# Summing the states of a state-space layer by accumulating transposes

## The chip, the cores and the metric

The kernel runs on one core of a Trainium2 chip. The metric is device time in microseconds. PE is the matrix engine (PEld its weight loads), DVE the vector engine, ACT the scalar engine, POOL is GpSimd and SP issues DMAs. An engine works through its own queue in order; semaphores tie the queues together.

## The reference

A small language model on 64 sequences of 128 tokens, 192 channels, all float32: embedding and layer norm, attention, a mixture of experts, a bidirectional state-space layer, a second mixture of experts, each added to the residual. The change is in the state-space layer:

```
xp, z = split(x @ W_in.T)                  # 384 channels each
xc = silu(causal_conv(xp, 4 taps) + conv_b)
dt, B, C = split(xc @ W_xproj.T)           # 12, 16, 16
dt = softplus(dt @ W_dt.T + b_dt);  A = -exp(A_log)
h[t] = exp(dt[t] * A) * h[t-1] + (dt[t] * xc[t]) * B[t]     # 384 x 16 states
y[t] = sum over the 16 states of h[t] * C[t]
y = (y + xc * D) * silu(z)
out = y @ W_out.T
layer = 0.5 * (forward over x + the same over x reversed)
```

## The kernel before

The phases follow one another; the state-space layer is `mamba_phase`. It works in 16 groups of 4 sequences (512 tokens). A group has a forward half (d = 0) and a backward half (d = 1), a half has 16 states n, and a state has three chunks c of 128 channels. The 48 pairs (n, c) of a half are its units, counted by p. Channels lie on the partitions, the 512 tokens along the free axis.

In each unit ACT writes the decays exp(dt A) into one of four PSUM banks (`act_decay`, L1760; `RING` says which), POOL has written u times B for the whole state into one of eight buffers xh (`pool_dBx`, L1804, two states ahead), and the DVE runs the recurrence as a scan (L1773). Then h is multiplied by C: for the states listed in `BY_POOL` (8 in the forward half, 6 in the backward half) POOL does it for the whole state in one call (`pool_read`, L1793), for the others the DVE does it chunk by chunk (`dve_read`, L1784). PE adds the product into the bank that holds y for the chunk, through a product with the identity (`pe_sum`, L1731), three states behind. D times xc goes into the same bank as a product with a diagonal matrix (`pe_D`, L1724). Both halves of a group add into these banks. When a group is complete, the DVE multiplies each chunk by silu(z) into ys (`dve_y`, L1811), PE multiplies ys by W_out (`pe_out`, L1743), and the DVE adds that to the residual H (`dve_out`, L1816).

While a half runs, the next half is prepared in between: `chain` puts the layer norm, the input product, the gate (L1561, L1562, copied by ACT at L1568), the convolution (L1579), the projection (L1599) and the softplus onto the engines at the units named in `POS`. The softplus ends in a loop over four engines. ACT makes e = exp(-|x|) (L1632) and two more tensors; POOL issues a DMA that adds e to r (`pool_add`, L1651); for each chunk PE sums three tensors through the identity (`pe_sp`, L1666), ACT copies the sum to dt (L1671), the DVE makes u = dt xc (L1675), and PE takes the next chunk only after u of the one before. One PSUM bank (`NB`) serves all these products. POOL needs u of all three chunks for the first product of the next half.

The order of each engine's queue is written out by hand: in each unit p first the main work, then what `POS` puts there (on PE what `POS` puts there first). POOL's main work in a state n is the product of state n+2, and then the read of state n-1 if it is POOL's.

Of the kernel before, what the change touches and what calls it, by code (L numbers as in the profile page):

```python
# [15 lines left out]
P = 128  # L16
# [3 lines left out]
G = 4  # L20
# [1334 lines left out]
def mamba_phase(nc, A, H, bank, K, Y, BCd, W):  # L1355
# [5 lines left out]
    with Phase(nc) as ctx:  # L1361
# [5 lines left out]
        POS = {  # L1367
            "y": (6, 7, 9), "pe_D0": (14, 15, 17), "pe_D1": (6, 16, 25), "pe_out": (17, 18), "out": (14, 15),
            "act_rows": (11, 13), "rows": (12, 14), "stats": 14, "rstd": 18, "norm": 40,
# [7 lines left out]
        NB = 7  # L1377
        BY_POOL = (0, 3, 4, 5, 10, 12, 13, 14), (0, 6, 9, 10, 11, 14)
        RING = ((3, 4, 5, 6) * 2 + (3, 4, 5, 3, 4, 5, 3) + (6, 4, 5, 3) * 8 + (6,),
# [54 lines left out]
        s_er, = ctx.software(K, 1)  # L1434
        s_gy, s_ops, s_out = sem("gated_ready"), sem("outps_ready"), sem("res_ready")

        def seqs(t):
# [24 lines left out]
        def act_gz(act, g):  # L1462
            act.wait_ge(s_zc, g * DC + DC)
            act.activation(gz[:, :, :], gz[:, :, :], ACT.Silu).then_inc(s_gz, 1)
# [8 lines left out]
        def chain(g, d, norm=True, first=False):  # L1473
# [57 lines left out]
            def act_zT(act, i):  # L1531
                if i == 0 and not first:
                    act.wait_ge(s_zps, gl * DC)
                act.wait_ge(s_zTps, gl * 2 + 1 + i)
                if i == 0:
                    act.copy(zTa[:, :], bank[:, front(i), :]).then_inc(s_zT, 1)
                else:
                    act.copy(zTb, bank[0:CR, front(i), :]).then_inc(s_zT, 1)
# [15 lines left out]

            def pe_gate(pe, c):
                if c == 0:
                    pe.wait_ge(s_abs, (s + 1) * 2 * DC)
                else:
                    pe.wait_ge(s_zc, g * DC + c)
                m = slice((DC + c) * P, (DC + c + 1) * P)  # L1560
                pe.matmul(bank[:, front(c), :], win_a[:, m], zTa[:, :], start=True, stop=False)  # L1561
                pe.matmul(bank[:, front(c), :], win_b[:, m], zTb, start=False, stop=True).then_inc(s_zps, 1)  # L1562

            def act_gate(act, c):
                act.wait_ge(s_zps, g * DC + c + 1)
                if c == 0 and deep:
                    act.wait_ge(s_gy, g * DC)
                act.copy(gz[:, c, :], bank[:, front(c), :]).then_inc(s_zc, 1)  # L1568

# [84 lines left out]
            def pe_sp(pe, c):  # L1654
                if c == 0:
                    if d == 1:
                        pe.wait_ge(s_zc, g * DC + DC)
                        stand_alone(pe, K.go)
                    pe.wait_ge(s_nc, s + 1)
                elif not first:  # L1660
                    pe.wait_ge(s_u, s * DC + c)
# [31 lines left out]
            for name, on_pe, on_act in stages:  # L1693
                if name == "x" and d == 1 or name == "gate" and d == 0:
                    continue
                for c in range(DC):
                    put("pe", POS[f"pe_{name}{d}"][c], on_pe, c)
                    put("act", POS[f"act_{name}{d}"][c], on_act, c)
# [19 lines left out]
        def pe_D(pe, g, d, c):  # L1718
            pe.wait_ge(s_xc, g * 2 + d + 1)
            if d == 0 and later(g):  # L1720
                pe.wait_ge(s_gy, (g - 1) * DC + c + 1)
            elif d == 0:
                pe.wait_ge(s_u, DC)
            pe.matmul(bank[:, c, :], dgD[:, c, :], xc[d][:, c, :], start=(d == 0), stop=False).then_inc(s_D, 1)  # L1724

        def pe_sum(pe, g, d, n, c):
            if n not in BY_POOL[d]:
                pe.wait_ge(s_prv, dve_reads(g, d, n) + c + 1)
            elif c == 0:
                pe.wait_ge(s_prp, pool_reads(g, d, n + 1))  # L1730
            mm = pe.matmul(bank[:, c, :], K.ident[:, :], xh[n % NX][:, c, :], start=False, stop=(d == 1 and n == NS - 1))  # L1731
            mm.then_inc(s_red, 1)

        def pe_out(pe, g, i):
            if i == 0:
                pe.wait_ge(s_gy, g * DC + DC)
                if not (isinstance(g, int) and g == NG - 1):
# [69 lines left out]
        def dve_y(dve, g, c):  # L1807
            dve.wait_ge(s_red, (g * 2 * NS + 2 * NS - 1) * DC + c + 1)
            if c == 0:
                dve.wait_ge(s_gz, g + 1)  # L1810
            dve.tensor_tensor(ys[:, c, :], bank[:, c, :], gz[:, c, :], ALU.mult).then_inc(s_gy, 1)  # L1811

# [84 lines left out]
        with nc.Block() as block:  # L1897
            @block.tensor
            def _(pe):
                def main(pe, g, d, p, end):  # L1900
                    carry = d == 0 and later(g)
                    if carry and p in POS["pe_D0"]:
                        pe_D(pe, g, d, POS["pe_D0"].index(p))
# [9 lines left out]
                def after(pe):  # L1913
                    for n in range(NS - LAG, NS):
                        for c in range(DC):
                            pe_sum(pe, NG - 1, 1, n, c)
                    for i in two:
                        pe_out(pe, NG - 1, i)
# [3 lines left out]
            def _(act):  # L1922
                def main(act, g, d, p, end):
                    act_decay(act, g, d, p)
                program(act, "act", main, lambda act: None, lambda act: None)

# [135 lines left out]
```

## Time and profile before

| | us |
|---|---|
| runs: median (lowest to highest of 3) | 4718.52 (4717.42 to 4736.08) |
| profiled execution, its span from first to last instruction | 4718.1 |
| PE busy | 4271.6 (91%) |
| DVE busy | 3251.1 (69%) |
| POOL busy | 3212.3 (68%) |
| ACT busy | 2430.7 (52%) |

The profile shows one execution. Busy time says how long an engine worked, not that it was needed: an engine that waits in order for another may be the last link of a loop although it has gaps. The state-space layer runs from about 1210 to 3818 us.

### The profile page before, as it was taken

The page shows a single profiled execution, that of the slowest core. Times are in us where ns is not written, and L with a number is a line of the kernel's source. Part 1 is how long each engine was busy: PE and PEld are TensorE (multiplying, and loading weights), DVE is VectorE, ACT ScalarE, POOL GpSimd, SP SyncE. Part 2 cuts the span into 40 slices and gives each one's busy share as a digit, 9 for nine tenths or more (in the row PEclk, how much of TensorE's full clock was granted, in tenths as well). Part 3 has the DMA queues.
Part 4 walks back from the last instruction along what each step waited for, and adds up shares of the span by engine and source line. Part 5 has one row for each costly group of instructions (what it writes and reads, how often), then busy time and mean ns, then how long its engine had stood idle before and what let it go on. Part 6 is the DMA issues. An engine that isn't in the chain of part 4 may idle for free. (4 is left out here: it accounts for less than half of the span.)

```text
span 4718.1 us, 62490 instructions
## 1 busy us (share of the span) xinstructions
PE 4271.6 (91%) x16896; PEld 2235.4 (47%) x16896; DVE 3251.1 (69%) x5016; ACT 2430.7 (52%) x4880; POOL 3212.3 (68%) x1669
## 2 busy tenths in 40 slices
PE   7999986997899999999999999999999876999994
PEld 4666644664343443344334434433443334666673
DVE  5667773111699999999999999989999975111114
ACT  3555542122566666767676666667666633222221
POOL 3222222442799999999999999999999941444441
PEclk9999996998899999999999999999999987999997
DMA  1000011342334333334333333333333321333456
GB/s 35 21 20 20 20 53 59 108 127 76 107 114 125 115 118 116 121 109 121 122 112 115 112 121 118 116 118 113 117 107 123 114 67 45 110 116 112 127 169 219
DMA packets 267113, 478.79 MB, mean 101 GB/s; under 512 B 39404, under 2 KB 176444, under 8 KB 266908
## 3 DMA queue, kind: packets, MB, share of 16 engines
q1 hardware_dynamic: 235776, 403.02, 26.9%
q0 software_dynamic: 28032, 73.17, 6.1%
q14 instruction: 171, 1.40, 0.1%
q10 hardware_dynamic: 3100, 0.64, 0.1%
q8 instruction: 34, 0.56, 0.1%
HBM read 409.75 MB, written 41.81 MB: 96 GB/s over the span
## 5 line engine op out<-in xcount | busy, mean ns | idle before, releaser
L1804 POOL TENSOR_TENSOR m_xh<-m_u,m_Bb 128x1536 f32<-128x1536 f32 x512 | 1780.1, 3550 | 51.6 <-DVE m_u L1675 39.0
L1731 PE MATMUL bank<-m_xh,ident 128*128 128x512 f32 x3072 | 1455.1, 609 | 34.3 <-POOL m_xh L1793 34.3
L1773 DVE TENSOR_TENSOR_SCAN bank<-bank,m_xh 128x512 f32<-128x512 f32 x864 | 1038.9, 1216 | 44.5 <-ACT bank L1760 42.2
L1760 ACT ACTIVATE bank<-m_dt,m_Ac 128x508 f32<-128x508 f32 x1536 | 1024.9, 683 | 38.4 <-DVE m_xh L1773 38.4
L1731 PEld LDWEIGHTS bank<-m_xh,ident 128*128 128x128 f32 x3072 | 576.2, 194 | 820.0 <-issue 730.7
L1773 DVE TENSOR_TENSOR_SCAN m_xh<-bank,m_xh 128x512 f32<-128x512 f32 x672 | 787.8, 1207 | 64.8 <-ACT bank L1760 59.3
L1793 POOL TENSOR_TENSOR m_xh<-m_xh,m_Cb 128x1536 f32<-128x1536 f32 x224 | 794.0, 3544 | 4.3 <-DVE m_xh L1773 4.0
L1784 DVE TENSOR_TENSOR m_xh<-bank,m_Cb 128x512 f32<-128x512 f32 x864 | 581.3, 673 | 10.9 <-DMA m_Cb<-BC_rows 10.8
L1204 ACT ACTIVATE f1t_h<-bank,f1t_b 128x512 f32<-128x512 f32 (+1 forms) x276 | 147.6, 586 | 509.9 <-PE bank L1234 509.9
L1134 POOL DMA_INDIRECT rows_y<-f1t_y,f1t_home x142 | 139.9, 985 | 316.4 <-DVE f1t_y L1175 287.1
L1579 PE MATMUL bank<-m_xp,m_dg 128*128 128x512 f32 x768 | 351.9, 601 | 3.7 <-DVE m_u L1675 1.4
L1243 PE MATMUL bank<-f1t_w,f1t_h 128*128 128x192 f32 x1704 | 289.0, 329 | 19.4 <-ACT f1t_h L1204 19.4
L1243 PEld LDWEIGHTS bank<-f1t_w,f1t_h 128*128 128x128 f32 x1704 | 275.7, 190 | 31.6 <-issue 28.1
L1759 ACT COPY bank<-m_none 128x4 f32<-128x4 f32 x896 | 144.2, 161 | 260.5 <-DVE m_xh L1784 171.3
L1164 DVE COPY f1t_xTa<-bank 128x512 f32<-128x512 f32 (+1 forms) x46 | 26.2, 570 | 342.2 <-PE bank L1215 342.2
L97 POOL TENSOR_SCALAR ln_e_ve<-ln_e_mv 128x4 f32<-128x4 f32 x16 | 3.7, 229 | 348.2 <-DVE ln_e_mv L91 348.2
L1579 PEld LDWEIGHTS bank<-m_xp,m_dg 128*128 128x128 f32 x768 | 142.9, 190 | 201.6 <-issue 157.0
L373 DVE TENSOR_REDUCE mx<-bank 128x3 f32<-128x384 f32 x256 | 141.0, 551 | 113.4 <-PE bank L552 112.1
L1231 PE MATMUL bank<-f1t_xTa,f1t_w1a 128*128 128x512 f32 (+1 forms) x552 | 217.1, 516 | 1.6 <-DVE f1t_xTb L1167 1.6
L1175 DVE TENSOR_TENSOR f1t_y<-bank,f1t_b 128x192 f32<-128x192 f32 x142 | 50.8, 358 | 216.7 <-PE bank L1243 216.7
L1204 ACT ACTIVATE f0t_h<-bank,f0t_b 128x512 f32<-128x512 f32 (+1 forms) x132 | 71.9, 596 | 246.5 <-PE bank L1234 246.5
L454 ACT COPY ST<-bank 128x384 f32<-128x384 f32 x256 | 120.8, 472 | 143.0 <-PE bank L562 143.0
(367 smaller groups left out, 6148.3 us busy)
## 6 DMA issues: line engine op xcount, KB each, us to landing
m_Bb<-BC_rows SPq DMA_DIRECT2D x256, 512.0 KB, 4.8
m_Cb<-BC_rows SPq DMA_DIRECT2D x256, 512.0 KB, 4.0
f1t_w<-f_w SPq DMA_DIRECT2D x46, 576.0 KB
m_r<-m_dt POOLq DMA_DIRECT2D x32, 768.0 KB, 7.4
f1t_w1a<-f_w SPq DMA_DIRECT2D x46, 384.0 KB
f0t_w<-f_w SPq DMA_DIRECT2D x22, 576.0 KB
f1c_yg<-rows_y SPq DMA_DIRECT2D x16, 768.0 KB, 8.3
f1t_w1b<-f_w SPq DMA_DIRECT2D x92, 96.0 KB
```

The lines of the kernel that those rows point to most:

```text
L373: dve.reduce_max(mx[:, u % NE, :], s_ps, AX).then_inc(s_mx, 1)
L1204: act.activation(h[b][:, m, 0:w * P], bank[:, HB[(s2 + m) % 4], 0:w * P], ACT.Gelu, bias=b1[b][:, m:m + 1]).then_inc(s_gelu, 1)
L1231: pe.matmul(o[f], w1a[b][:, (m + f) * P:(m + f + 1) * P], xTa[b][:, 0:w * P], start=True, stop=False)
L1243: mm = pe.matmul(bank[:, YB[j % 2], 0:C], h[b][:, m, j * P:(j + 1) * P], w2[b][:, m, :], start=(m == 0), stop=(m == HK - 1))
L1579: mm = pe.matmul(bank[:, front(c), :], dg[:, c, k, :], xp[:, c, :, o:o + P], start=(k == 0), stop=(k == TAPS - 1))
L1731: mm = pe.matmul(bank[:, c, :], K.ident[:, :], xh[n % NX][:, c, :], start=False, stop=(d == 1 and n == NS - 1))
L1759: act.copy(o[:, :, edge:edge + 1], none[:, :].unsqueeze(2))
L1760: act.activation(o[:, :, lo:hi], seqs(dt[d][:, c, :])[:, :, lo:hi], ACT.Exp, scale=Ac[:, c, n:n + 1]).then_inc(s_dA, 1)
L1773: dve.tensor_tensor_scan(o, bank[:, RING[d][p], way], xh[n % NX][:, c, way], 0.0, ALU.mult, ALU.add).then_inc(s_h, 1)
L1784: dve.tensor_tensor(xh[n % NX][:, c, :], bank[:, RING[d][p], :], Cb[q % RC][:, n % QN, :], ALU.mult).then_inc(s_prv, 1)
L1793: pool.tensor_tensor(v, v, Cb[q % RC][:, n % QN, :].unsqueeze(1).to_broadcast([P, DC, TOK]), ALU.mult).then_inc(s_prp, 1)
L1804: pool.tensor_tensor(xh[n % NX][:, :, :], u[d][:, :, :], Bb[q % RB][:, n % QN, :].unsqueeze(1).to_broadcast([P, DC, TOK]), ALU.mult).then_ ...
```

## The change

The sum over the states is turned. PE now takes each 128 x 128 block of the product as the stationary operand and adds its transpose into the bank, so that y lies with tokens on the partitions and channels along the free axis. D is added in that layout (xc stationary, the diagonal matrix moving), and the gate is computed in it (z's tokens stationary, W_in moving, one step for each of the four sequences). The DVE multiplies y by the gate in place in gz. Since the output product needs channels on the partitions, PE then turns the gated product back (`pe_yT`) and ACT copies it to ys (`act_yT`). The waits on ys move from `s_gy` to the new semaphore `s_ys`. GpSimd reads out 7 and 5 states instead of 8 and 6: state 13 of the forward half and state 10 of the backward half go to the DVE.

```diff
@@ -1365,17 +1365,17 @@
         POS = {
-            "y": (6, 7, 9), "pe_D0": (14, 15, 17), "pe_D1": (6, 16, 25), "pe_out": (17, 18), "out": (14, 15),
+            "y": (6, 7, 9), "pe_yT": (8, 9, 11), "act_yT": (10, 11, 13), "pe_D0": (14, 15, 17), "pe_D1": (6, 16, 25), "pe_out": (17, 18), "out": (14, 15),
             "act_rows": (11, 13), "rows": (12, 14), "stats": 14, "rstd": 18, "norm": 40,
             "pe_zT": (43, 46), "act_zT": (44, 45), "pe_x0": (0, 1, 2), "act_x0": (0, 1, 4), "pe_conv0": (3, 4, 5),
-            "act_conv0": (6, 10, 12), "pe_conv1": (0, 2, 4), "act_conv1": (1, 4, 7), "pe_gate1": (23, 26, 31), "act_gate1": (25, 27, 30),
+            "act_conv0": (6, 10, 12), "pe_conv1": (0, 2, 4), "act_conv1": (1, 4, 7), "pe_gate1": (23, 25, 27, 31), "act_gate1": (24, 26, 28, 32),
             "pe_dt0": (12, 14, 16), "act_dt0": (17, 20, 22), "pe_dt1": (20, 21, 22), "act_dt1": (19, 21, 22), "pe_pj": (10, 11),
...
         NB = 7
-        BY_POOL = (0, 3, 4, 5, 10, 12, 13, 14), (0, 6, 9, 10, 11, 14)
+        BY_POOL = (0, 3, 4, 5, 10, 12, 14), (0, 6, 9, 11, 14)
         RING = ((3, 4, 5, 6) * 2 + (3, 4, 5, 3, 4, 5, 3) + (6, 4, 5, 3) * 8 + (6,),
@@ -1433,6 +1433,7 @@
         s_gy, s_ops, s_out = sem("gated_ready"), sem("outps_ready"), sem("res_ready")
+        s_yT, s_ys = sem("gated_turned"), sem("gated_copied")
 
@@ -1460,7 +1461,7 @@
         def act_gz(act, g):
-            act.wait_ge(s_zc, g * DC + DC)
+            act.wait_ge(s_zc, g * G + G)
             act.activation(gz[:, :, :], gz[:, :, :], ACT.Silu).then_inc(s_gz, 1)
@@ -1530,7 +1531,7 @@
                 if i == 0 and not first:
-                    act.wait_ge(s_zps, gl * DC)
+                    act.wait_ge(s_zps, gl * G)
                 act.wait_ge(s_zTps, gl * 2 + 1 + i)
@@ -1552,20 +1553,20 @@
 
-            def pe_gate(pe, c):
-                if c == 0:
+            def pe_gate(pe, j):
+                if j == 0:
                     pe.wait_ge(s_abs, (s + 1) * 2 * DC)
                 else:
-                    pe.wait_ge(s_zc, g * DC + c)
-                m = slice((DC + c) * P, (DC + c + 1) * P)
-                pe.matmul(bank[:, front(c), :], win_a[:, m], zTa[:, :], start=True, stop=False)
-                pe.matmul(bank[:, front(c), :], win_b[:, m], zTb, start=False, stop=True).then_inc(s_zps, 1)
-
-            def act_gate(act, c):
-                act.wait_ge(s_zps, g * DC + c + 1)
-                if c == 0 and deep:
-                    act.wait_ge(s_gy, g * DC)
-                act.copy(gz[:, c, :], bank[:, front(c), :]).then_inc(s_zc, 1)
+                    pe.wait_ge(s_zc, g * G + j)
+                o, sl = bank[:, NB, 0:DC * P], slice(j * P, (j + 1) * P)
+                pe.matmul(o, zTa[:, sl], win_a[:, DC * P:2 * DC * P], start=True, stop=False)
+                pe.matmul(o, zTb[:, sl], win_b[:, DC * P:2 * DC * P], start=False, stop=True).then_inc(s_zps, 1)
+
+            def act_gate(act, j):
+                act.wait_ge(s_zps, g * G + j + 1)
+                if j == 0 and deep:
+                    act.wait_ge(s_yT, g * DC)
+                act.copy(gz[:, :, j * P:(j + 1) * P], bank[:, NB, 0:DC * P].rearrange("p (c x) -> p c x", c=DC)).then_inc(s_zc, 1)
 
@@ -1654,7 +1655,7 @@
                     if d == 1:
-                        pe.wait_ge(s_zc, g * DC + DC)
+                        pe.wait_ge(s_zc, g * G + G)
                         stand_alone(pe, K.go)
@@ -1693,7 +1694,7 @@
                     continue
-                for c in range(DC):
+                for c in range(G if name == "gate" else DC):
                     put("pe", POS[f"pe_{name}{d}"][c], on_pe, c)
@@ -1718,22 +1719,39 @@
             if d == 0 and later(g):
-                pe.wait_ge(s_gy, (g - 1) * DC + c + 1)
+                pe.wait_ge(s_ys, (g - 1) * DC + c + 1)
             elif d == 0:
                 pe.wait_ge(s_u, DC)
-            pe.matmul(bank[:, c, :], dgD[:, c, :], xc[d][:, c, :], start=(d == 0), stop=False).then_inc(s_D, 1)
+            for j in range(G):
+                sl = slice(j * P, (j + 1) * P)
+                mm = pe.matmul(bank[:, c, sl], xc[d][:, c, sl], dgD[:, c, :], start=(d == 0 and j == 0), stop=False, skip_group_check=True)
+            mm.then_inc(s_D, 1)
 
...
                 pe.wait_ge(s_prp, pool_reads(g, d, n + 1))
-            mm = pe.matmul(bank[:, c, :], K.ident[:, :], xh[n % NX][:, c, :], start=False, stop=(d == 1 and n == NS - 1))
+            for j in range(G):
+                sl = slice(j * P, (j + 1) * P)
+                mm = pe.matmul(bank[:, c, sl], xh[n % NX][:, c, sl], K.ident[:, :], is_transpose=True, start=False,
+                               stop=(d == 1 and n == NS - 1), skip_group_check=True)
             mm.then_inc(s_red, 1)
+
+        def pe_yT(pe, g, c):
+            pe.wait_ge(s_gy, g * DC + c + 1)
+            for j in range(G):
+                sl = slice(j * P, (j + 1) * P)
+                mm = pe.transpose(bank[:, c, sl], gz[:, c, sl], K.ident[:, :])
+            mm.then_inc(s_yT, 1)
+
+        def act_yT(act, g, c):
+            act.wait_ge(s_yT, g * DC + c + 1)
+            act.copy(ys[:, c, :], bank[:, c, :]).then_inc(s_ys, 1)
 
...
             if i == 0:
-                pe.wait_ge(s_gy, g * DC + DC)
+                pe.wait_ge(s_ys, g * DC + DC)
                 if not (isinstance(g, int) and g == NG - 1):
@@ -1808,7 +1826,7 @@
                 dve.wait_ge(s_gz, g + 1)
-            dve.tensor_tensor(ys[:, c, :], bank[:, c, :], gz[:, c, :], ALU.mult).then_inc(s_gy, 1)
+            dve.tensor_tensor(gz[:, c, :], bank[:, c, :], gz[:, c, :], ALU.mult).then_inc(s_gy, 1)
 
@@ -1899,6 +1917,8 @@
                     carry = d == 0 and later(g)
+                    if carry and p in POS["pe_yT"]:
+                        pe_yT(pe, g - 1, POS["pe_yT"].index(p))
                     if carry and p in POS["pe_D0"]:
@@ -1914,6 +1934,8 @@
                             pe_sum(pe, NG - 1, 1, n, c)
+                    for c in range(DC):
+                        pe_yT(pe, NG - 1, c)
                     for i in two:
@@ -1922,7 +1944,13 @@
                     act_decay(act, g, d, p)
-                program(act, "act", main, lambda act: None, lambda act: None)
+                    if d == 0 and later(g) and p in POS["act_yT"]:
+                        act_yT(act, g - 1, POS["act_yT"].index(p))
+
+                def after(act):
+                    for c in range(DC):
+                        act_yT(act, NG - 1, c)
+                program(act, "act", main, lambda act: None, after)
 
```

## Rows read from the trace of the kernel before

**Rows 1.** The page's first line.

```profile
span 4718.1 us, 62490 instructions
```

**Rows 2.** Windows over the state-space phase; the sum and mean of 16 stretches.

```profile
core 0: us, PE busy (x) PEld busy (x) DVE busy (x) ACT busy (x) POOL busy (x), PEclk, DMA share, GB/s
...
sum 2608.00, PE 2495.93 PEld 1035.06 DVE 2390.08 ACT 1727.46 POOL 2555.50; mean PE 156.00 PEld 64.69 DVE 149.38 ACT 107.97 POOL 159.72
```

**Rows 3.** Groups by line and shape, 1860 to 3480 us: busy us, mean ns | idle before.

```profile
L1804 POOL TENSOR_TENSOR m_xh<-m_u,m_Bb 128x1536 f32<-128x1536 f32 x319 | 1109.7, 3552 | 20.4 <-DVE m_u L1675 11.6 <-PE bank L1731 8.7
...
L1784 DVE TENSOR_TENSOR m_xh<-bank,m_Cb 128x512 f32<-128x512 f32 x537 | 361.3, 673 | 5.4 <-DMA m_Cb<-BC_rows 5.3
...
L1568 ACT COPY m_gz<-bank 128x512 f32<-128x512 f32 x30 | 17.5, 584 | 6.6 <-PE bank L1562 6.4
```

**Rows 4.** Timeline of the DVE: start us, us, instruction, count [idle before <-releaser].

```profile
1875.74 0.69 DVE L1811 TENSOR_TENSOR m_r<-bank,m_gz 128x512 f32<-128x512 f32 x1 [1.86 <-PE bank L1731]
...
2338.13 0.69 DVE L1675 TENSOR_TENSOR m_u<-bank,m_xc 128x512 f32<-128x512 f32 x1
...
2399.17 0.67 DVE L1784 TENSOR_TENSOR m_xh<-bank,m_Cb 128x512 f32<-128x512 f32 x1
2399.76 1.22 DVE L1773 TENSOR_TENSOR_SCAN bank<-bank,m_xh 128x512 f32<-128x512 f32 x1
...
2420.76 0.69 DVE L1675 TENSOR_TENSOR m_u<-bank,m_xc 128x512 f32<-128x512 f32 x1 [1.71 <-ACT m_dt L1671]
...
2501.70 0.69 DVE L1675 TENSOR_TENSOR m_u<-bank,m_xc 128x512 f32<-128x512 f32 x1 [0.16 <-ACT m_dt L1671]
...
2687.47 0.69 DVE L1811 TENSOR_TENSOR m_r<-bank,m_gz 128x512 f32<-128x512 f32 x1 [1.78 <-PE bank L1731]
```

**Rows 5.** Timeline of POOL, 2336 to 2503 us.

```profile
2336.36 10.41 POOL L1804 TENSOR_TENSOR m_xh<-m_u,m_Bb 128x1536 f32<-128x1536 f32 x3
2346.57 3.61 POOL L1793 TENSOR_TENSOR m_xh<-m_xh,m_Cb 128x1536 f32<-128x1536 f32 x1
...
2396.50 0.90 POOL L1651 DMA_DIRECT2D m_r<-m_dt  x1
...
2421.75 3.44 POOL L1804 TENSOR_TENSOR m_xh<-m_u,m_Bb 128x1536 f32<-128x1536 f32 x1 [0.51 <-DVE m_u L1675]
...
2473.55 0.88 POOL L1651 DMA_DIRECT2D m_r<-m_dt  x1
...
2502.67 3.45 POOL L1804 TENSOR_TENSOR m_xh<-m_u,m_Bb 128x1536 f32<-128x1536 f32 x1 [0.81 <-DVE m_u L1675]
```

**Rows 6.** Timeline of ACT, e of the softplus.

```profile
2467.14 1.48 ACT L1632 ACTIVATE m_dt<-m_dt 128x1536 f32<-128x1536 f32 x1
```

**Rows 7.** Waits, 1860 to 3480 us (ten groups): us in total, times, longest.

```profile
ACT m_dt L1671 <- PE bank L1666: 165.0, 59, 5.0
```

**Rows 8.** Timeline of PE: softplus sums, state sums, transposes, products of 70 columns.

```profile
2411.36 1.02 PE L1666 MATMUL bank<-m_u,ident 128*128 128x512 f32 x2
...
2413.08 1.02 PE L1666 MATMUL bank<-m_r,ident 128*128 128x512 f32 x2
2413.94 3.60 PE L1731 MATMUL bank<-m_xh,ident 128*128 128x512 f32 x8
...
2421.60 0.63 PE L1528 MATMUL bank<-ident,m_z 128*128 128x128 f32 x4 [0.63 <-DVE m_u L1675]
...
2481.09 1.99 PE L1666 MATMUL bank<-m_r,ident 128*128 128x512 f32 x2 [3.53 <-DMA m_r<-m_dt]
...
747.90 27.37 PE L1037 MATMUL bank<-f0v_marked,f0v_at_lo 128*128 128x70 f32 x127 [13.29 <-DVE f0v_at_lo L1000]
```

**Rows 9.** Windows, granted clock third from last: PE alone; all engines; L562's transposes alone.

```profile
2481.00:2483.50 2.50, 2.41 (x3) 0.53 0.27 110
...
750.00:755.00 5.00, 5.00 (x25) 5.00 (x25) 1.88 (x2) 2.82 (x12) 0.00 (x0) 0.50 0.02 3
...
155.00:255.00 100.00, 22.67 (x129) 15.13 (x129) 0.98 0.07 20
```

## The prediction

> **What bounds the kernel now.** I read the page first: the span is 4718.1 us [rows 1]. The windows by stretch come next: the state-space phase fills 2608 us, and cut into 16 stretches of 163 us on the mean, about a group each, it has POOL busy 159.7, PE 156.0 and DVE 149.4 us, ACT only 108 [rows 2]. So three engines are near full, and an average can't say which one paces. The groups by line give the prices [rows 3]: one POOL call on a state (three chunks of 512) takes 3.55 us, one DVE read of a chunk 0.673. The timelines give the order. From the first gated product of one group to that five groups later the DVE takes 811.73 us, 162.35 a group [rows 4], and that is the number to move.
>
> Why 162.35? The softplus hides a loop through all engines. POOL issues the DMA that adds into r; PE needs r for the first softplus sum; ACT copies it and meanwhile issues no decays; the DVE waits for decays and for u; POOL can't begin the next half's products before u's third chunk. In the cycle that I follow, third u chunks begin at 2338.13, 2420.76 and 2501.70: half A (82.6 us) and half B (80.9 us) [rows 4]. On POOL both halves are nearly gapless: calls start every 3.40 us, from (10.21 / 3) [rows 5], and the r DMA is issued at 2396.50 and 2473.55 in the middle of the queue. In half B ACT had e ready at 2467.14 + 1.48 = 2468.6 [rows 6], so the DMA stood 4.9 us behind POOL's earlier calls. POOL waits only 0.5 and 0.8 us for u at the half's end [rows 5]: POOL and the softplus loop finish together.
>
> PE is late too, but through its queue: ACT waits 165 us in ten groups for softplus sums behind other work [rows 7]. The DVE waits 1.71 us for the third u chunk of half A, and 1.86 (first of six groups) to 1.78 us (last) for the first gated product [rows 4].
>
> **Part by part, for one group.**
> (1) GpSimd. Readouts of state 13 forward and state 10 backward leave POOL: 2 x 3.40 = 6.80 us. By the issue order (the product of state n+2, then the read of n-1) both belong to half B: the read of 13 stands behind the first product of the next half, the read of 10 behind the DMA. Half A keeps its 23 calls: 23 x 3.40, the DMA 0.7 and the layer norm's small steps, some 2.3 = 81.2 us. In half B the DMA comes one call, 3.40 us, earlier.
> (2) DVE. Six more reads at the spacing of a read, 2399.76 - 2399.17 = 0.59 us [rows 4]: 3.5 us. Busy becomes 152.9 of 162.35. In half B three reads (state 10) lie between the r DMA and the third u chunk, on the loop: +1.77. One of state 13's lies before half A's last chunk, where POOL is later anyway; two open half B, +1.2, within the 4.9 - 3.40 = 1.5 us that ACT's e still has in hand before the DMA.
> (3) PE sums. Now 2 records per sum, spaced (3.60 - 0.61) / 7 = 0.43 us [rows 8]: 0.855 a sum, 96 sums 82 us. New: four 128-column transposes. The program's own transposes are one record each, four of them 0.63 us; with 0.28 for the last, a spacing of 0.117 [rows 8]. Four make 0.47, 96 sums 45 us, a saving of 37. Bounds: 0.28 x 4 = 1.12 a sum if they don't overlap at all (25 us more than now, which would make PE the bound), and 0.855 if accumulating transposes run as two passes like a plain float product. I take 0.47, the same operation in the same phase.
> (4) D: 4 products of 128 columns, two records each; 8 x 0.117 = 0.94 against 0.855 (no overlap: 8 x 0.28 = 2.24), six a group, +0.5 us of PE (up to +8). The gate: 6 x 2 records of 512 columns become 8 x 2 of 384, the same columns. The turn back of y: 12 transposes, 1.4 us. PE's sum: 156.0 - 37 + 0.5 + 1.4 = 121 us.
> (5) ACT: three new copies of 128x512 at 0.584, as the gate's copies [rows 3], 1.75 us; four gate copies of 384 columns instead of three of 512 (same elements, one more start, below 0.6 us). ACT has 54 us idle.
> (6) Waits. PE now waits for the gated product before each turn, ACT for the turn, PE's D for the copy. Behind PE's wait stand the last sum, the projection and D; behind ACT's copies the decays of units 11 to 13. Through D and the output product the DVE's residual add may come about 1 us later than now. All of it lies in the first part of half A, before the r DMA, where POOL's queue is the later one. It costs nothing as long as that holds, about 1 us a group when it doesn't. DMAs, SP's queue and the waits for B and C rows are unchanged in count; C rows are released by the reader of the state, sooner or later by under a call.
>
> **Sum.** Half A: POOL still has 81.2 us; with 0.3 for the hop from u to POOL 81.6 (now 82.6 here). Softplus in A gains more than this (the 1.71 us wait goes with PE's backlog), but POOL holds it. Half B: 80.94 - 3.40 (call) + 1.77 (reads) - 0.7 (small waits for u behind PE's queue) = 78.6; if PE also starts r's sum at full clock, 0.9 less, 77.7. This sum took 1.99 us in half B at 2481.09 against the usual 1.02 (at 2413.08), after PE had waited 3.53 us for the DMA, with a granted clock of 0.53 in that stretch, the 1.2 GHz level for most of it [rows 8, 9]. So a cycle of 159.3 to 160.2, say 159.85 against the mean 162.35: 2.5 us. Over 15 cycles 38 us. The last half, all POOL's, loses two calls (6.8 us), of which the DVE's reads give back half, and the drain gains a turn and a copy: -3 net, an estimate from the same prices. 4718.1 - 38 - 3 = 4677 us. Span and run agree (4718.1 against the median 4718.52), so the 0.4 us around the span is kept as nothing.
>
> **The clock.** PE will have some 40 us of slack a group in place of 6, in short gaps. In this trace a wait of 3.5 us was followed by 0.53 [rows 9]. A run of products of 70 columns, each with a new 128-column load, stayed at 1.2 GHz (0.50) although PE was never idle in its 27.37 us (127 records, 0.216 apart) [rows 8, 9]. New sums also load 128 columns for each 128 that they move. Against it: the attention stage gives 22.67 of 100 us to transposes and is granted 0.98 [rows 9]. But there they lie among products, so the row decides nothing about long runs. The Trainium skill, page "TensorE: Matmul & The Clock Gate", section "Part 4: PE-mode transpose", says that the full clock does not come on for transposes. By that rule sum runs would go at 1.2 GHz and the fourth rival below would hold; no run here shows it for a transpose yet.
>
> **Rivals.**
> Second: the DVE becomes the bound and gives the gain back. For it: it takes over 3.5 us, and of its 13 us idle only the two waits on PE (1.8 and 1.71) are plainly PE's: 162.35 + 3.5 - 3.5 gives 162.35, with the drain 4717. Against it: its waits in half B follow from the late DMA, which comes earlier.
> Third: POOL was the only bound, and all 6.8 us show: 15 x 6.8 + 4 = 106, 4612. Against it: half A keeps its 23 calls.
> Fourth, slower: PE at 1.2 GHz in the softplus stretches. Its place is the loop: the second and third softplus sums are 2.58 us each at full clock (2411.36 to 2413.94 [rows 8]) and wait for the u before them, so at half rate each adds 2.58 us to the loop. Half A: 5.1 more, less some 2 that its loop has in hand against POOL once the 1.71 us wait is gone, +3; half B: +5. 159.85 + 8 = 168, +5.5 a group against now, 4718 + 83 = 4800. It decides from 2.5 us a group on, that is when nearly half of these sums run slow. If PE ran slow all the time, (156 - 82) x 2 + 96 x 0.94 = 238 us a group, far above; the worst end, which I don't reach, since bursts of plain products follow in each half.
> Fifth: accumulating transposes cost two passes. PE stays at 158; only POOL's call and the DVE's reads count, some 1.6 us a group, 4695.
>
> **How the numbers follow.** Forecast 0.44 (own range 4655 to 4700), second 0.20, third 0.14, fourth 0.16, fifth 0.06. Within 0.5% (4694.5 to 4741.7), about what a measurement can tell from no change: a tenth of the first, most of the second and half of the fifth. Faster: nine tenths of the first, all of the third, rest of the fifth and some of the second, 0.59. Slower: most of the fourth, 0.15. Same: 0.26. The range reaches from between the third and the first to the foot of the fourth: 4625 to 4750.
>
> **What would show it.** Right: 32 + 12 POOL calls a group, half A still about 81 us with gapless POOL, half B below 79; sum records near 0.117 us apart; PE near 121 us busy a group; the wait of the first gated product for PE gone. Wrong: granted clock well below 0.9 in this phase with softplus sums near 5 us; or DVE busy above 155 us a group with POOL waiting for scans; or two records per transpose.

## The result, and the profile after

The changed kernel takes 4796.39 us (median, 4794.92 to 4799.32) against 4723.32 for the kernel before (four runs, the three of the table above and one more): ratio 1.0155, 95% interval 1.0142 to 1.0168. It is slower by 73 us, where 38 + 3 us less were forecast. In the profiled executions the spans are 4793.6 and 4718.1 us [rows 1], 75.5 apart.

The page of the kernel after: the busy line and the clock that TensorE was granted, in 40 slices.

```profile
span 4793.6 us, 70708 instructions
...
PE 3905.7 (81%) x20800; PEld 2516.5 (52%) x20800; DVE 3303.5 (69%) x5112; ACT 2480.3 (52%) x5040; POOL 3113.2 (65%) x1637
...
PEclk9999997997898989998899988989999877999997
```

Windows of the kernel after over the state-space phase, the sum and mean of 16 stretches of a group each, which answers to [rows 2]:

```profile
sum 2685.00, PE 2129.53 PEld 1317.16 DVE 2444.14 ACT 1778.42 POOL 2455.99; mean PE 133.10 PEld 82.32 DVE 152.76 ACT 111.15 POOL 153.50
```

POOL fell by 6.2 us a group and the DVE rose by 3.4, both as forecast (two calls less, six reads more). PE fell by 22.9, not 35. No engine fills its stretch of 167.8 us as POOL did before: POOL is busy for 91% of it, where it was 98%.

Timeline of the DVE after (start, duration, instruction, idle before it): the first gated products four groups apart, and u's chunks in the cycle from 2378 to 2547 us. It answers to [rows 4].

```profile
1899.47 0.69 DVE L1829 TENSOR_TENSOR m_gz<-bank,m_gz 128x512 f32<-128x512 f32 x1 [0.98 <-PE bank L1737]
...
2378.39 0.68 DVE L1676 TENSOR_TENSOR m_u<-bank,m_xc 128x512 f32<-128x512 f32 x1
...
2449.83 0.69 DVE L1676 TENSOR_TENSOR m_u<-bank,m_xc 128x512 f32<-128x512 f32 x1 [3.38 <-ACT m_dt L1672]
...
2463.74 0.69 DVE L1676 TENSOR_TENSOR m_u<-bank,m_xc 128x512 f32<-128x512 f32 x1 [1.30 <-ACT m_dt L1672]
...
2546.76 0.68 DVE L1676 TENSOR_TENSOR m_u<-bank,m_xc 128x512 f32<-128x512 f32 x1
...
2569.05 0.69 DVE L1829 TENSOR_TENSOR m_gz<-bank,m_gz 128x512 f32<-128x512 f32 x1 [0.97 <-PE bank L1737]
```

A group takes (2569.05 - 1899.47) / 4 = 167.4 us, 5.05 more than before; fifteen cycles make 75.8, the whole loss. Half A (third u chunk of B to third of A) is 85.4 us, half B 83.0; before they were 82.6 and 80.9. New is the wait of 3.38 us for the first u chunk of half A.

Timelines of PE and ACT after, the same place: the fourth gate copy and the first softplus sum of half A (three pairs of records), and for PE the first pair of the third sum.

```profile
2437.74 0.91 PE L1563 MATMUL bank<-m_low_w,m_low 64*128 64x384 f32 x2
2438.58 0.66 PE L1737 MATMUL bank<-ident,m_xh 128*128 128x128 f32 x4
2443.86 2.04 PE L1667 MATMUL bank<-m_u,ident 128*128 128x512 f32 x2 [4.62 <-ACT m_gz L1569]
2445.69 1.92 PE L1667 MATMUL bank<-m_lw,ident 128*128 128x512 f32 x2
2447.40 1.77 PE L1667 MATMUL bank<-m_r,ident 128*128 128x512 f32 x2
...
2458.54 1.53 PE L1667 MATMUL bank<-m_u,ident 128*128 128x512 f32 x2 [2.43 <-DVE m_u L1676]
```

```profile
2438.09 1.47 ACT L1645 ACTIVATE m_lw<-m_u 128x1536 f32<-128x1536 f32 x1
2439.59 1.57 ACT L1647 ACTIVATE m_u<-m_u,ones 128x1536 f32<-128x1536 f32 x1
...
2443.24 0.47 ACT L1569 COPY m_gz<-bank 128x384 f32<-128x384 f32 x1
...
2449.21 0.59 ACT L1672 COPY m_dt<-bank 128x512 f32<-128x512 f32 x1 [3.59 <-PE bank L1667]
```

PE has the fourth gate product done by 2438.7, but ACT's copy of it stands at unit 32, behind the logarithm, its companion and decays. PE stands for 4.62 us, and then needs 5.2 us for a sum that took 2.6 at full clock [rows 8]. ACT waits 3.59 us for that sum and issues no decays.

Windows of the kernel after (busy time of each engine; the granted clock is the third number from the end): a run of state sums, PE's wait, the softplus sum behind it.

```profile
core 0: us, PE busy (x) PEld busy (x) DVE busy (x) ACT busy (x) POOL busy (x), PEclk, DMA share, GB/s
2376.10:2379.70 3.60, 3.60 (x34) 3.60 (x33) 3.60 (x6) 2.75 (x7) 0.36 (x1) 1.00 0.05 19
2439.30:2443.80 4.50, 0.00 (x0) 0.00 (x0) 4.50 (x6) 4.38 (x9) 4.50 (x2) 0.81 0.90 231
2443.90:2449.10 5.20, 5.20 (x7) 2.10 (x8) 2.54 (x3) 1.39 (x3) 5.20 (x3) 0.52 0.54 209
```

The clock falls during the wait and is 0.52, nearly all at the 1.2 GHz level, while the sum runs.

Waits after, 1876 to 3546 us (ten groups): us in total, times, longest.

```profile
POOL m_xh L1822 <- PE bank L1737: 80.8, 51, 4.2
...
DVE bank L1791 <- ACT bank L1778: 64.8, 42, 3.3
...
DVE m_u L1676 <- ACT m_dt L1672: 44.8, 20, 3.9
PE bank L1667 <- ACT m_gz L1569: 42.4, 10, 4.6
```

PE's wait for the gate copy comes ten times in ten groups. POOL, relieved of two calls, now waits 8.1 us a group for PE to free state buffers, where it was 0.9 [rows 3]; some 4 us of that stand at the head of half A, where u's third chunk too ends only 0.3 us before POOL goes on.

### The profile page after: what moved, and what is told of

Read it like the earlier page. It is cut to its first block and busy times, and to the rows that moved or that the text cites. A ratio compares the mean times of both kernels' runs of the same rounds, so it can differ in the third digit from the quotient of the medians.

```text
span 4793.6 us, 70708 instructions
## 1 busy us (share of the span) xinstructions
PE 3905.7 (81%) x20800; PEld 2516.5 (52%) x20800; DVE 3303.5 (69%) x5112; ACT 2480.3 (52%) x5040; POOL 3113.2 (65%) x1637
## 5 line engine op out<-in xcount | busy, mean ns | idle before, releaser
L1791 DVE TENSOR_TENSOR_SCAN bank<-bank,m_xh 128x512 f32<-128x512 f32 x960 | 1153.7, 1215 | 98.3 <-ACT bank L1778 98.3
L1737 PEld LDWEIGHTS bank<-ident,m_xh 128*128 128x128 f32 x6144 | 744.8, 150 | 311.8 <-issue 228.9
L1737 PE MATMUL bank<-ident,m_xh 128*128 128x128 f32 x6144 | 839.6, 288 | 47.8 <-POOL m_xh L1811 40.7
L1811 POOL TENSOR_TENSOR m_xh<-m_xh,m_Cb 128x1536 f32<-128x1536 f32 x192 | 665.9, 3468 | 63.1 <-DVE m_xh L1791 62.1
L1791 DVE TENSOR_TENSOR_SCAN m_xh<-bank,m_xh 128x512 f32<-128x512 f32 x576 | 682.6, 1208 | 27.2 <-ACT bank L1778 22.9
L1802 DVE TENSOR_TENSOR m_xh<-bank,m_Cb 128x512 f32<-128x512 f32 x960 | 644.0, 671 | 2.6 <-DMA m_Cb<-BC_rows 2.6
L1580 PE MATMUL bank<-m_xp,m_dg 128*128 128x512 f32 x768 | 389.9, 654 | 105.1 <-ACT m_xc L1588 94.7
L1777 ACT COPY bank<-m_none 128x4 f32<-128x4 f32 x992 | 159.4, 161 | 421.4 <-DVE m_xh L1802 311.7
L1667 PE MATMUL bank<-m_u,ident 128*128 128x512 f32 x192 | 142.4, 833 | 202.3 <-DVE m_u L1676 96.7
```

The costliest lines, as they stand in the source:

```text
L1580: mm = pe.matmul(bank[:, front(c), :], dg[:, c, k, :], xp[:, c, :, o:o + P], start=(k == 0), stop=(k == TAPS - 1))
L1667: mm = pe.matmul(bank[:, front(c), :], K.ident[:, :], t[:, c, :], start=(k == 0), stop=(k == 2))
L1737: mm = pe.matmul(bank[:, c, sl], xh[n % NX][:, c, sl], K.ident[:, :], is_transpose=True, start=False, stop=(d == 1 and n == NS - 1), skip_ ...
L1777: act.copy(o[:, :, edge:edge + 1], none[:, :].unsqueeze(2))
L1791: dve.tensor_tensor_scan(o, bank[:, RING[d][p], way], xh[n % NX][:, c, way], 0.0, ALU.mult, ALU.add).then_inc(s_h, 1)
L1802: dve.tensor_tensor(xh[n % NX][:, c, :], bank[:, RING[d][p], :], Cb[q % RC][:, n % QN, :], ALU.mult).then_inc(s_prv, 1)
```

## The experiments

Each ratio is to the kernel before on the same chip (medians of 4724.6 to 4725.8 us), with its 95% interval.

**Which part loses.** One part of the change at a time was undone or done alone.

e1_turned_reads14, the changed kernel with the old readouts:

```
-        BY_POOL = (0, 3, 4, 5, 10, 12, 14), (0, 6, 9, 11, 14)
+        BY_POOL = (0, 3, 4, 5, 10, 12, 13, 14), (0, 6, 9, 10, 11, 14)
```

> The changed kernel with GpSimd's old list of readouts (8 forward, 6 backward): the DVE's six extra reads (3.5 us a group) are gone, the turned layout stays. If the reads are the loss (the DVE paces), a group falls from 167.4 us to about 162.4 to 164 and the time to 4717 to 4745 us. If TensorE's turned work is the loss (its low clock in the softplus sums and the late fourth gate copy), a group stays at 166 to 168 and the time at 4775 to 4800. If only GpSimd's relief had held the change back from being worse, it gets slower than 4796.

Measured 4786.82, ratio 1.0133 (1.0112 to 1.0155): 10 us better than the change (the two intervals touch), 61 still missing. The reads are no more than a small part.

e2_old_layout_reads12, the same line the other way round in the kernel before:

> The kernel before with the new list of readouts alone (7 forward, 5 backward), sums in the old layout. If the reads are the loss (the DVE paces), a group grows by 2 to 3.5 us and the time to 4748 to 4770 us. If the prediction's account of GpSimd's queue holds and the turned layout is the loss, about 1.6 us a group are gained: 4690 to 4700.

Measured 4735.19, ratio 1.0023 (1.0012 to 1.0033): 10 us worse and outside both expectations: less than the 2 us a group that the reads alone were to cost at least, and no sign of the gain that the prediction put on the readouts. The other 61 us come with the turned layout.

e3_gate_early, the changed kernel with its last gate unit two units earlier:

```
-  ... "pe_gate1": (23, 25, 27, 31), "act_gate1": (24, 26, 28, 32),
+  ... "pe_gate1": (23, 25, 27, 29), "act_gate1": (24, 26, 28, 30),
```

> The changed kernel with the last two gate units moved earlier: TensorE's fourth gate product from unit 31 to 29, ACT's copies at 24, 26, 28, 30 instead of 24, 26, 28, 32, so that the first softplus sum of half A is freed as early as before the change. If the late gate copy holds the loop in half A, the DVE's wait of 3.4 us at the first u chunk goes and a group falls by 2.5 to 3.4 us: 4745 to 4760. If the clock or the DVE's reads are the loss, under 1 us a group: 4780 to 4800.

Measured 4737.94, ratio 1.0031 (1.0021 to 1.0041): 58 us of the 73 are gone, more than expected. PE's timeline and clock in the same place:

```profile
2416.09 1.10 PE L1667 MATMUL bank<-m_u,ident 128*128 128x512 f32 x2 [2.28 <-ACT m_gz L1569]
2417.02 1.02 PE L1667 MATMUL bank<-m_lw,ident 128*128 128x512 f32 x2
2418.18 1.10 PE L1667 MATMUL bank<-m_r,ident 128*128 128x512 f32 x2
```

```profile
2416.10:2419.30 3.20, 3.06 (x8) 1.26 (x9) 3.20 (x5) 2.60 (x6) 3.20 (x2) 1.00 0.60 161
```

The wait is 2.28 us instead of 4.62, and behind it the sum runs at full clock. The DVE's waits for u in half A are gone, here and in the other groups. So far this can be the lateness or the clock.

e4_products_not_transposes, `is_transpose=True` taken out of the state sums:

> The changed kernel with each accumulating transpose made an ordinary float product with the identity as moving side (the form that its D already has): same layout, same waits, same result, two records where the transpose has one. TensorE's sums go from 0.44 us to about 0.9 us and its busy time by some 40 us a group. If the light load lets the clock fall and that is the loss, the granted clock goes back to 0.97 or more, the softplus sums to 0.34 us a record, and the time to 4720 to 4760. If the clock is no cause, TensorE's queue is again full and the time stays at 4796 or grows to 4830.

Measured 4894.11, ratio 1.0358 (1.0335 to 1.0381), worse than any expectation. The granted clock over ten groups was 0.98, but PE was busy 1575 of 1670 us, a sum took 1.0 us, and the first gated product waited 3.1 us for PE. The full queue cost more than the clock could give back, so the run doesn't decide on the clock; it does show that the transposes themselves save PE time.

**Lateness or clock.** e5_before_gate_late puts the kernel before's last gate copy where the change had its own:

```
-  ... "act_gate1": (25, 27, 30),
+  ... "act_gate1": (25, 27, 32),
```

> The kernel before (old layout, old readouts) with one number changed: ACT's third and last gate copy at unit 32 instead of 30, where the change put its own last one. If the place of the last gate copy alone costs what the early gate won back (58 us), the time grows to 4755 to 4780 us and the DVE waits 2.5 to 3.5 us a group at the first u chunk of half A. If only the turned layout is sensitive to it, the time stays within 15 us of before.

Measured 4725.43, ratio 0.9999 (0.9990 to 1.0009). The place of the copy alone costs nothing. In the old layout PE is itself late there: it waits only 0.95 us for the copy, and the sum behind runs in 1.10 and 1.02 us a pair.

e9_late_gate_warm_wait, the changed kernel with its late gate and products that add zero, in the wait (`zw` is a bf16 tile that is set to zeros once, at the start):

```
                     if d == 1:
+                        for _ in range(14):
+                            pe.matmul(bank[:, 0, :], zw[:, 0:P], zw[:, :], start=False, stop=False, skip_group_check=True)
                         pe.wait_ge(s_zc, g * G + G)
```

> The changed kernel with its late gate as it is, and 14 bf16 products of zeros (512 columns, 3.0 us at full clock, 6.0 at half) on TensorE just ahead of its wait for the fourth gate copy; they add nothing to y. TensorE would stand idle there for 4.6 us. If the fall of the clock during the wait is half of the cost (the softplus sums that follow took 2.04, 1.92, 1.77 us for a pair instead of 1.02), the pair goes back to about 1.02, 2 to 2.6 us a group come back and the time is 4755 to 4770. If the late copy alone is the cost, 4785 to 4800; if the added products hold the sums up, above 4800.

Measured 4745.79, ratio 1.0046 (1.0028 to 1.0064): 50.6 us better than the change, more than expected, with the copy as late as it was. PE's timeline and clock:

```profile
2415.91 3.19 PE L1661 MATMUL bank<-m_zw 128*128 128x512 bf16 x14
2420.70 1.10 PE L1671 MATMUL bank<-m_u,ident 128*128 128x512 f32 x2 [1.60 <-ACT m_gz L1571]
2421.63 1.02 PE L1671 MATMUL bank<-m_lw,ident 128*128 128x512 f32 x2
2422.49 1.02 PE L1671 MATMUL bank<-m_r,ident 128*128 128x512 f32 x2
```

```profile
2420.70:2423.40 2.70, 2.70 (x7) 1.19 (x8) 2.58 (x3) 1.39 (x3) 2.70 (x2) 1.00 0.63 155
```

The copy comes 3.19 + 1.60 = 4.8 us behind PE's last useful work, as in the change, but the sum runs at 1.00. The DVE's wait at the first u chunk is 0.9 us instead of 3.4, the one at the third is gone. In all ten groups the pair behind this wait takes 1.10 us, where the change takes 1.69 to 2.05. So of the 58 us that the early gate gives back, some 50 are the fall of the clock in the wait. The 8 between this run and e3 may be the lateness itself, but the two intervals overlap.

e7_gate_early_warm, a product of zeros ahead of every state sum of e3:

```
+            pe.matmul(bank[:, c, :], zw[:, 0:P], zw[:, :], start=False, stop=False, skip_group_check=True)
             for j in range(G):
```

> The turned layout with the early gate, and ahead of each accumulated state a bf16 product of zeros (512 columns) into the same bank: it adds nothing to y, keeps TensorE's columns moving and costs it about 0.21 us each, 20 us a group of its 35 us of slack. If the low clock is a part of what is left, the granted clock goes from 0.92 to 0.96 or more, the softplus products fall from 0.63 to 0.69 us to about 0.6, and 1 to 3 us a group come back: 4690 to 4725. If the DVE's own 153 us with its short waits paces, nothing comes back: 4733 to 4750.

Measured 4733.40, ratio 1.0025 (1.0015 to 1.0035). The clock over ten groups rose to 0.97, and no more than the interval's width came back. So the rest of the low clock is hidden, or the added products (PE busy 1476 of 1670 us instead of 1347) took back what it gave. This run says nothing of r's sum in half B: PE still stands for the DMA there, and the pair behind it took 2.04 or 2.05 us in all ten groups, as in e3.

**What is left.** e6_gate_early_reads14 is e3 with the old readouts, e8_gate_early_reads13 with 8 and 5 of them.

> The turned layout with the early gate and the old list of readouts (8 and 6). If the two costs found so far add up (early gate -58 us, old readouts -10 us from 4796), about 4728. If TensorE's 35 us of relief a group is worth something once the gate is early, 4690 to 4715. If GpSimd, gapless again, paces: 4725 to 4745, with GpSimd busy 159 to 160 us of a group and the DVE idle 13 us.

> The turned layout with the early gate and 13 states a group read out by GpSimd (8 forward, 5 backward): three reads fewer on the DVE (1.77 us a group), one call more on GpSimd (3.4). If the DVE paces, 10 to 25 us less than with 12: 4713 to 4728. If GpSimd paces half A's loop, 4738 or more.

Measured 4744.25 (ratio 1.0038, 1.0026 to 1.0051) and 4742.34 (1.0034, 1.0023 to 1.0045), against 4737.94 with 12: the intervals overlap. The two costs don't add up: with the early gate, fewer reads on the DVE help no longer. Nor does the DVE alone pace, which would have given 4713 to 4728 in e8. The trace of e3 shows where the DVE still stands, in half B; timelines of PE, ACT and the DVE:

```profile
2495.43 2.05 PE L1667 MATMUL bank<-m_r,ident 128*128 128x512 f32 x2 [3.99 <-DMA m_r<-m_dt]
```

```profile
2497.52 0.58 ACT L1672 COPY m_dt<-bank 128x512 f32<-128x512 f32 x1 [4.65 <-PE bank L1667]
```

```profile
2498.72 1.23 DVE L1791 TENSOR_TENSOR_SCAN bank<-bank,m_xh 128x512 f32<-128x512 f32 x1 [3.30 <-ACT bank L1778]
```

ACT stands 4.65 us in order at unit 30 for r's sum, which waits for the DMA; the u chunk that needs the copy comes at unit 34. e10_gate_early_sp0_late moves that copy:

```
-  ... "act_sp0": (30, 39, 41),
+  ... "act_sp0": (33, 39, 41),
```

> The early gate kernel with ACT's copy of half B's first softplus sum at unit 33 instead of 30, so that ACT issues three more decays before it stands waiting for r's DMA; the u chunk that needs it comes at unit 34. The DVE's wait of 3.30 us for decays in that place should go. If the DVE now paces (153 us busy and its short waits), a group falls by 2 to 3.3 us: 4690 to 4710. If what is saved there comes back as a wait for u a few units later, or GpSimd paces, 4730 to 4740.

Measured 4690.37, ratio 0.9921 (0.9903 to 0.9938): better than both kernels. Its DVE timeline:

```profile
1877.12 0.69 DVE L1829 TENSOR_TENSOR m_gz<-bank,m_gz 128x512 f32<-128x512 f32 x1 [0.97 <-PE bank L1737]
...
2336.11 0.67 DVE L1676 TENSOR_TENSOR m_u<-bank,m_xc 128x512 f32<-128x512 f32 x1
...
2416.17 0.67 DVE L1676 TENSOR_TENSOR m_u<-bank,m_xc 128x512 f32<-128x512 f32 x1
...
2496.25 0.67 DVE L1676 TENSOR_TENSOR m_u<-bank,m_xc 128x512 f32<-128x512 f32 x1
...
2518.68 0.69 DVE L1829 TENSOR_TENSOR m_gz<-bank,m_gz 128x512 f32<-128x512 f32 x1 [0.98 <-PE bank L1737]
```

A group takes (2518.68 - 1877.12) / 4 = 160.4 us, both halves of the one shown 80.1.

**Which part gains.** The same late copy in the kernel before (e11_before_sp0_late), in the old layout with 12 readouts (e12_old_layout_reads12_sp0_late), and e10 with 14 (e13_turned_reads14_both):

> The kernel before with the same one number changed (ACT's copy of half B's first softplus sum at unit 33 instead of 30). If GpSimd, busy 159.7 of 162.35 us, paces the kernel before, at most 1 us a group comes of it: 4705 to 4725. If the DVE's waits pace it too, 2 to 3 us a group: 4675 to 4695.

> The old layout with 12 states read out by GpSimd and ACT's copy of half B's first softplus sum at unit 33. If the readouts make the gain, as the prediction's sum has it, about 4690. If the gain needs TensorE's relief, since TensorE is busy 156 of 162 us in the old layout and takes GpSimd's place as the bound, 4715 to 4735.

> The turned layout with the early gate and the late copy, but the old 14 readouts on GpSimd. If TensorE's relief makes the gain, 4685 to 4700. If GpSimd's 160 us of calls then pace again, 4720 to 4740, and the gain needs both parts.

Measured 4725.42 (ratio 1.0002, 0.9991 to 1.0013), 4731.29 (1.0018, 1.0009 to 1.0028) and 4728.32 (1.0004, 0.9987 to 1.0021). Only both parts together gain, and they only with ACT's copy moved (e3 has both, and 4737.94). Windows over 1876 to 3546 us, the sums of e11, e12, e13 and e10 in this order:

```profile
sum 1670.00, PE 1614.87 PEld 671.05 DVE 1531.07 ACT 1119.49 POOL 1637.40; mean PE 1614.87 PEld 671.05 DVE 1531.07 ACT 1119.49 POOL 1637.40
```

```profile
sum 1670.00, PE 1612.75 PEld 669.49 DVE 1565.05 ACT 1129.86 POOL 1569.68; mean PE 1612.75 PEld 669.49 DVE 1565.05 ACT 1129.86 POOL 1569.68
```

```profile
sum 1670.00, PE 1375.90 PEld 855.63 DVE 1532.87 ACT 1138.25 POOL 1638.57; mean PE 1375.90 PEld 855.63 DVE 1532.87 ACT 1138.25 POOL 1638.57
```

```profile
sum 1670.00, PE 1368.70 PEld 852.02 DVE 1591.72 ACT 1171.64 POOL 1600.24; mean PE 1368.70 PEld 852.02 DVE 1591.72 ACT 1171.64 POOL 1600.24
```

With the old parts POOL is busy 98% and PE 97% of the time. The readouts free POOL and leave PE at 97% (e12); the layout frees PE and leaves POOL at 98% (e13). With both (e10) the DVE, at 95%, and POOL, at 96%, are the fullest; that these two now share the bound is read from the shares, no run shows it.

e14_both_warm_r keeps PE's clock up ahead of r's sum in half B of e10 (14 products of zeros before the wait for the DMA), and e15_both_y_out_later moves the end of the group:

```
-  "y": (6, 7, 9), "pe_yT": (8, 9, 11), "act_yT": (10, 11, 13), ... "out": (14, 15),
+  "y": (7, 8, 10), "pe_yT": (9, 10, 12), "act_yT": (11, 12, 14), ... "out": (15, 16),
```

> The 4690 us kernel with 14 bf16 products of zeros (512 columns) on TensorE ahead of its wait for r's DMA in half B, where it stands idle for some 4 us and then runs r's sum in 2.05 us for the pair. If the low clock there still costs, the pair falls to about 1.1 and 0.9 us a group come back: 4675 to 4680. If the late copy's place has already hidden it, 4686 to 4694.

> The 4690 us kernel with the DVE's gated products one unit later (7, 8, 10 for 6, 7, 9), the turns and their copies one unit later too, and the residual adds at 15, 16 for 14, 15. If the DVE paces and its waits of 0.98 us for y and 1.14 us for the output product are what the new order costs, 1.5 to 2 us a group come back: 4660 to 4670. If they come back as waits elsewhere, 4685 to 4695.

Measured 4689.44 (ratio 0.9924, 0.9907 to 0.9941) and 4725.63 (1.0003, 0.9993 to 1.0014). In e14 the pair of r fell to between 1.02 and 1.10 us, and nothing came of it: once ACT's copy is late enough, the half rate of that sum costs nothing. e15 lies outside both expectations. The DVE's wait for y went, but the waits for ACT's decays rose from 4.5 to 8.9 us a group (31.2 + 13.4 and 51.0 + 37.7 in ten), and PE's D products, which stayed at their units, now wait 2.2 us a group for the turned copies. The end of the group can't be moved without what follows it.

## Why the prediction was wrong

The time fell in the fourth rival: PE at 1.2 GHz in the softplus stretches, 4800. Its size was nearly right, its account only in part, so that the nearness (4800 against 4796) is in part luck. Of its signs of being wrong one came, a softplus sum near 5 us (5.2, the first of half A), while the clock of the whole phase, 0.89, is hardly below 0.9.

- **Steps (5) and (6) failed.** Step (5) priced the gate by its elements ("one more start, below 0.6 us"), and (6) put all new waits in the first part of half A and let them "cost nothing". Neither followed the fourth gate unit to whom it frees: PE's first softplus sum of half A waits for ACT's last gate copy, and the change set that copy from unit 30 to 32 while it made PE earlier by its saved sums. The wait was 4.62 us a group, and it lies on the loop. [Rows 8, 9] had the price: after 3.53 us of waiting r's sum ran at half rate. The prediction put that row into its sum for half B alone.
- **The fourth rival's mechanism** was right in kind and price (a sum at half rate costs some 2.6 us more), wrong in its reach: not the second and third sums of both halves but the first sum of half A, and part of the third (1.53, 1.91, 1.51 us a pair). Nor was it the light load in all of the group: with PE busy for 1347 of 1670 us and the clock at 0.92, e3 has 58 of the 73 us back, and e7, at 0.97, is no faster than e3 beyond its interval.
- **Half B's term (-3.40 + 1.77 - 0.7) failed.** In e3, with the gate mended, half B (2432.56 to 2517.01) is 84.5 us, and 83.4 to 84.5 in ten groups, not 78.6. The DMA did not come a call earlier: it was issued 54.1 us after half A's third u chunk, against 52.8 before [rows 4, 5]. ACT had e ready at 50.2 (47.9 before), so e was not what held it. POOL's queue was: it has one call of 3.4 us less there, but it stood 3.4 us in front of others, mostly for PE to free state buffers, and began the half 1.7 us later. A timeline of POOL in e3:

```profile
2471.47 3.45 POOL L1822 TENSOR_TENSOR m_xh<-m_u,m_Bb 128x1536 f32<-128x1536 f32 x1 [2.02 <-PE bank L1737]
2475.67 3.44 POOL L1822 TENSOR_TENSOR m_xh<-m_u,m_Bb 128x1536 f32<-128x1536 f32 x1 [0.75 <-PE bank L1737]
2479.34 3.46 POOL L1811 TENSOR_TENSOR m_xh<-m_xh,m_Cb 128x1536 f32<-128x1536 f32 x1 [0.23 <-DVE m_xh L1791]
2483.22 3.48 POOL L1822 TENSOR_TENSOR m_xh<-m_u,m_Bb 128x1536 f32<-128x1536 f32 x1 [0.42 <-PE bank L1737]
2486.65 0.85 POOL L1652 DMA_DIRECT2D m_r<-m_dt  x1
```

Then r's sum ran at half rate in all ten groups of e3, in five of ten before, and ACT stood at unit 30 for it. With ACT's copy moved (e10) half B is 80.1, although the DMA comes as late (2469.79 - 2416.17 = 53.6).

- **Half A's term was right within 2 us once the gate was early**: 80.1 measured in e10 and 80.0 in e3, 81.6 forecast; in the changed kernel it is 85.4. Its reason was not right: POOL does not fill half A but stands 4.2 us (e3) and 2.4 us (e10) at its head.
- **The bound was half seen.** The prediction held that POOL and the softplus loop finish together and gave PE's saving no value of its own. e12 shows that without the turned layout nothing is gained; that it is PE's saving in that layout which counts is read from the busy shares.
- **The second rival** (the DVE gives the gain back) has the first undoing of the reads for it, 10 us, but not the second: in e6 against e3 it is 6 the other way. Both differences are hardly larger than the intervals.
- **The sums were priced right.** The transposes come one record each, (3.66 - 0.28) / 31 = 0.109 us apart in a run of 32 (0.117 forecast), by this row of PE's timeline after:

```profile
2376.05 3.66 PE L1737 MATMUL bank<-ident,m_xh 128*128 128x128 f32 x32
```

The fifth rival is out. The window over this run has the clock at 1.00, which products ahead of it could still have left. A run of 40 behind r's sum in half B of the kernel after tells more; its row in PE's timeline, and two windows inside it:

```profile
2527.06 6.20 PE L1737 MATMUL bank<-ident,m_xh 128*128 128x128 f32 x40
```

```profile
2527.60:2530.60 3.00, 3.00 (x16) 3.00 (x15) 2.13 (x3) 2.33 (x6) 3.00 (x2) 0.50 0.48 149
2531.00:2533.20 2.20, 2.20 (x21) 2.02 (x19) 2.20 (x4) 0.89 (x3) 2.20 (x2) 1.00 0.73 276
```

The clock is at 0.50 in the first window and at 1.00 in the second, and PE did nothing but transposes from the one to the other. The Trainium skill, page "TensorE: Matmul & The Clock Gate", section "Part 4: PE-mode transpose", says that the full clock does not engage for transposes; by these rows it does here, and the measurement decides.

PE's 133 us a group against 121 forecast are in part the products at half rate: on the mean of ten groups the softplus records took 0.85, 0.84 and 0.68 us and those of the convolution 0.65, where one of either takes 0.59 at full clock.

What stays open: whether fewer reads on the DVE really help with the late gate (e1, 10 us) and not with the early one (e6), as both differences are near the noise. POOL at 97.5% busy in e6 speaks for POOL, but no run took that apart. Open too is what sets the time at which PE's sums free the state buffers that POOL now waits for.

## What to carry to other kernels

When a change makes one engine lighter, list each wait in its queue again: it now arrives earlier, so what used to be late because of it becomes what it stands waiting for, and here TensorE paid for 4.6 idle microseconds a second time, with a sum at half rate. A position in a hand-written order belongs to the load that it was tuned for; before giving up on a part, move the producer that the new wait names. Where two engines are both above 95% busy, try their relief together: here each alone gained nothing.

## What the runs showed of the hardware

TensorE's granted clock behind a wait: 1.00 after waits of 1.60 (e9) and 2.28 us (e3), 0.52 after 4.62 (after). The length of the last wait alone does not decide it. After 2.43 us the third sum of half A ran at 1.00 in e9 and at 0.57 in the changed kernel. And in the kernel before, r's sum took 1.10 us after a wait of 3.78 and 1.99 after one of 3.53. Fourteen bf16 products of zeros, 3.19 us, ahead of the wait kept the clock at 1.00 behind it (e9), though their data are zeros. While PE ran nothing but transposes it rose from 0.50 to 1.00 (after).
